# A written-out drain, one gather buffer per batch, and the maximum's scores first, in a one-core attention and mixture-of-experts kernel

## The reference

```python
x = x + tanh(g_xattn[0]) * attention(layernorm(x), ctx, ctx)     # 16 batches, 256 x 256, 16 heads of 16
xf = layernorm(x)                                                # 4096 tokens of 256
scores = softmax(xf @ w_router);  weights, indices = top_k(scores, 2)      # 8 experts
moe    = sum over the two experts of weight * (silu(xf @ w1) * (xf @ w3)) @ w2   # hidden 512
shared = silu(xf @ ws1) * (xf @ ws3) @ ws2
x = x + tanh(g_ffn[0]) * (shared / 3 + moe * 2 / 3)
```

## Time and profile before

| | |
|---|---|
| runs | 934.19, 934.75, 927.93 us, median 934.19 |
| profiled execution | 931.92 us |
| its span (first to last instruction) | 930.2 us |
| mean granted clock of PE | 0.948 |
| busy | PE 818.6 (88%), PEld 727.7, DVE 535.9 (58%), ACT 418.0 (45%), POOL 378.9 (41%) |

### The profile page before, as it was taken

How to read it: one execution, slowest core, us unless ns; L and a number is a source line. 1 busy time by engine, 2 the same in 40 slices (tenths; PEclk the granted TensorE clock), 3 DMA queues, 4 the chain that set the end, 5 groups by cost and what they waited for, 6 DMA issues and landing times.

```text
span 930.2 us, 19000 instructions
## 1 busy us (share of the span) xinstructions
PE 818.6 (88%) x7106; PEld 727.7 (78%) x7107; DVE 535.9 (58%) x1104; ACT 418.0 (45%) x691; POOL 378.9 (41%) x373
## 2 busy tenths in 40 slices
PE   2478999999999998878899999999999999968765
PEld 2365777677777766558799999999999999968765
DVE  4256788888888878554843444444343433535545
ACT  5228776666666655644333333333333333311211
POOL 4524446555555532325660513135051300345571
PEclk9759999999999989789999999999999999988887
DMA  4869877778888886324575413143241111234352
GB/s 147 236 129 190 202 165 209 191 189 186 206 197 191 172 172 170 132 93 164 181 250 196 133 57 124 56 124 112 69 132 60 56 57 45 86 97 129 122 153 73
DMA packets 103409, 131.47 MB, mean 141 GB/s; under 512 B 9904, under 2 KB 87472, under 8 KB 103344
## 3 DMA queue, kind: packets, MB, share of 16 engines
q1 hardware_dynamic: 91696, 93.37, 40.3%
q0 software_dynamic: 11648, 37.23, 12.1%
HBM read 75.25 MB, written 55.05 MB: 140 GB/s over the span
## 4 chain that ended last, share of the span: by engine, by line
PE 62%; DVE 18%; issue 8%; DMA 3%; ACT 3%; another core or an unknown queue 3%; SPq 1%; POOL 1%; DVEq 0%; ACTq 0%; POOLq 0%
PE bank L499 7%; PE bank L501 6%; PE bank L500 6%; DVE row_max L1178 6%; PE bank_sm L499 5%; PE bank_sm L501 5%; PE bank_sm L500 5%; PE bank_ss L499 4%; PE bank_ss L501 4%; PE bank_ss L500 4%; PE bank_sm L592 4%; PE bank_ss L581 3%; PE bank L608 3%; PE bank L517 2%
## 5 line engine op out<-in xcount | busy, mean ns | idle before, releaser
L1178 DVE TENSOR_REDUCE row_max<-bank_sm 128x4 f32<-128x1024 f32 x128 | 156.3, 1221 | 70.3 <-PE bank_sm L592 47.1
L820 ACT ACTIVATE probs_T<-bank_ss 128x1024 f32<-128x1024 f32 x128 | 131.6, 1028 | 38.7 <-PE bank_ss L581 37.3
L499 PE MATMUL bank_sm<-xg_h,w_h 128*128 128x256 f32 x400 | 119.9, 300 | 30.7 <-DVE xg_l L1052 27.6
L1052 DVE TENSOR_TENSOR gT_l<-gg,gT_h 128x1024 fp32r<-128x1024 f32 x50 | 80.8, 1616 | 95.2 <-ACT gT_h L946 90.7
L501 PE MATMUL bank_sm<-xg_l,w_h 128*128 128x256 f32 x400 | 118.6, 296 | 0.0
L500 PE MATMUL bank_sm<-xg_h,w_l 128*128 128x256 f32 x400 | 118.4, 296 | 0.0
L499 PE MATMUL bank<-w_h,gT_h 128*128 128x256 f32 x400 | 114.6, 287 | 3.2 <-DVE x_all L1289 3.2
L499 PE MATMUL bank_ss<-xg_h,w_h 128*128 128x256 f32 x400 | 116.8, 292 | 0.0
L501 PE MATMUL bank<-w_l,gT_h 128*128 128x256 f32 x400 | 114.3, 286 | 0.7 <-issue 0.7
L500 PE MATMUL bank<-w_h,gT_l 128*128 128x256 f32 x400 | 114.6, 286 | 0.4 <-issue 0.4
L500 PE MATMUL bank_ss<-xg_h,w_l 128*128 128x256 f32 x400 | 113.1, 283 | 0.0
(11 more groups left out here) (173 smaller groups left out, 2015.0 us busy)
## 6 DMA issues: line engine op xcount, KB each, us to landing
qk_d<-qk_s SPq DMA_DIRECT2D x32, 512.0 KB, 7.7
w_raw<-wall POOLq DMA_DIRECT2D x27, 512.0 KB, 3.9
k<-qk_d SPq DMA_DIRECT2D x96, 128.0 KB, 4.4
q<-qk_d SPq DMA_DIRECT2D x96, 128.0 KB, 6.4
xg<-xs_d SPq DMA_DIRECT2D x35, 256.0 KB, 2.7
ys_d<-y_s SPq DMA_DIRECT2D x34, 256.0 KB, 2.2
x<-x SPq DMA_DIRECT2D x16, 256.0 KB
c_s<-ctxT SPq DMA_DIRECT2D x16, 256.0 KB, 3.2
```

What stands on the lines that cost most here:

```text
L499: pe.matmul(out, ah, bh, start=first and k == 0, stop=False)
L820: act.activation(pT[:, 2 * (pv % 4):2 * (pv % 4) + 2, :].rearrange("p h t -> p (h t)"), SS[:, :], ACT.Exp, scale=D ** -0.5).then_inc(exp_o ...
L1052: return v.tensor_tensor(dst, ps, high.bitcast(F32), ALU.subtract)
L1178: v.tensor_reduce(mx[B.slot][:, :, :].rearrange("p t (r q) -> p r t q", r=2)[:, :, :, p], SM[:, :].rearrange("p (r t k) -> p r t k", r=2, ...
```

## The change

- **Order of the drain.** `iterations` now ends at i = NB - 1. What is left of the batches 13, 14 and 15 (x13, x14, x15) is written out in a row on each engine, with the pieces of the shared tiles between them; the tables UP1, UP3 and DOWN go. For that the steps became functions of their own.
- **Work moved out of the drain.** ACT's copy w_h0 is at i = NB - 3, DVE's `w_l` and the first `xg_l` are in slots 0 to 3 of i = NB - 1. `router_exp` of the last three batches, and the sums of scores and router weights that need it, come behind tile 6's g_high and g_low (three buffers instead of one hold their input and output). POOL's cut of the first expert's weights has its last part behind the last scatter.
- **Slots.** PE issues the maximum's scores first, the exponential's second.
- **Router on DVE.** slot_i is cast ahead of slots_all; score_sum, its reciprocal and the weights come at the end, each waiting for the one before.
- **Gathers.** `yg` has room for all 16 batches (in the place of the experts' weights, which are used up), with a semaphore for each batch. The 64 gathers are issued in a row, with one `carry`.
- **Mixes and SP's queue.** The mixes come one tile later: 0 and 1 in tile 9, 12 and 13 in tile 15. Ahead of the stores of tile j - 2's mixes stands the load of tile j, so the loads run a tile further ahead.

```diff
-    for i in range(-AHEAD, NB + 3):
+    for i in range(-AHEAD, NB):
...
 def mixed_at(j):
-    if j == NB - 1:
-        return ()
-    first = 2 * (min(j, NB - 1) - EARLY - 2)
-    return range(max(0, first), NB if j == NB else max(0, first + 2))
+    first = max(0, 2 * (min(j, NB) - EARLY - MIX_FROM))        # MIX_FROM = 3
+    return range(first, min(NB, max(0, 2 * (j + 1 - EARLY - MIX_FROM))) if j < NB else NB)
...
 SP
     for j in range(EARLY + 2, NB):
         load_shared(j, total + (j - 1))
-        for b in mixed_at(j - 1):
+        for b in mixed_at(j - 2):
             store_out(b)
...
 PE
         for p in range(PAIRS):
-            scores(p)
+            if B:
+                scores_to_max(B, p)
+            V, pv = late_pair(C, S, p)
+            if V:
+                scores_to_exp(V, pv)
...
+    scores_to_exp(x15, PAIRS - 2)
+    values(x15, 2)
+    up1(0, SHARED)
+    scores_to_exp(x15, PAIRS - 1)
+    logits(x13)
+    values(x15, 3)
+    project_out(x14)
+    rank(x13, rk_tail)
+    attention_rows(x15)
+    up3(0, SHARED)
+    turn_out(x15)
+    turn_norm(x14)
+    up1(1, SHARED)
+    logits(x14)
+    project_out(x15)
+    rank(x14, rk_tail)
+    up3(1, SHARED)
+    down(0, SHARED)
+    turn_norm(x15)
+    up1(2, SHARED)
+    logits(x15)
+    up3(2, SHARED)
+    rank(x15, rk_tail)
+    down(1, SHARED)
...
 ACT
+            if i == SPLIT_AT and p in (1, 3, 5):               # SPLIT_AT = NB - 3
+                n = p // 2
+                act.wait_ge(w_in[n], 16)
+                act.activation(w_h0[:, part(n)], wraw[:, part(n)], ACT.Copy).then_inc(w_used, 1)
...
+    for b in (x13, x14, x15):
+        router_exp(b)
...
 DVE
+            if i == NB - 1 and p in (0, 1, 3):
+                n = (0, 1, None, 2)[p]
+                v.wait_ge(w_used, n + 1)
+                v.tensor_tensor(w_l0[:, part(n)], wraw[:, part(n)], w_h0[:, part(n)].bitcast(F32), ALU.subtract).then_inc(w_ok, 1)
+            if i == NB - 1 and p == 2:
+                x_low_shared(0, 0)
...
     def mix(b):
-        n, turn = b % RG, b // RG
-        v.wait_ge(yg_in[n], turn * 64 + 64)
+        v.wait_ge(yg_in[b], 64)
...
 POOL
+    scatter(x14)
+    cut(1, 0, which=(0, 1))
+    scatter(x15)
+    cut(1, 0, which=(2,))
...
+    carry(NB)
     for b in range(NB):
-        n = b % RG
-        moved(po, mix_ok, b - RG + 1)
-        carry(NB + b)
         for t in range(TS):
-            for k, dst in enumerate((yga, ygb)):
+            for k in range(2):
                 po.indirect_dma_start(
-                    out=dst[n][:, t, :], out_offset=None, in_=ys_d,
+                    out=yg[:, b, k, t, :], out_offset=None, in_=ys_d,
```

More of the change, by code:

```diff
@@ L219, in build @@
             ysh = sb(m, "y_shared", [P, EARLY, TS * E])
[L221 to L226, removed]
+            with ExitStack() as w:
+                w_h, w_l = [], []
+                for i in range(2):
+                    w_h.append(sb(w, f"w_h{i + 1}", [P, WSZ], F32R))
+                    w_l.append(sb(w, f"w_l{i + 1}", [P, WSZ], F32R))
+                w_h.append(w_h0)
+                w_l.append(w_l0)
+            yg = sb(m, "y_gathered", [P, NB, 2, TS, E])
             x2a = sb(m, "x2_all", [P, NB, TS * E])
@@ new lines, in scores_to_exp @@
+            def scores_to_exp(V, pv):
+                if pv == 0:
+                    pe.wait_ge(mrow, V.n(32, 32))
+                moved(pe, exp_ok, V.n(PAIRS, pv))
+                for half in range(TC):
+                    for par in range(2):
+                        own = slice(ROWS * par, ROWS * par + ROWS)
+                        r = pe.matmul(SS[:, par * 512 + half * L:par * 512 + (half + 1) * L],
+                                      k4[V.slot][own, pv, half * P:(half + 1) * P], q4[V.slot][own, pv, :],
+                                      start=True, stop=True)
+                r.then_inc(ss_ps, 1)
@@ new lines, in scores_to_max @@
+            def scores_to_max(B, p):
+                if p == 0:
+                    pe.wait_ge(stk[B.slot], B.turn * 192 + 192)
+                moved(pe, mx_ok, B.n(PAIRS, p))
+                for half in range(TC):
+                    for par in range(2):
+                        own = slice(ROWS * par, ROWS * par + 3 * D)
+                        r = pe.matmul(SM[:, par * 512 + half * L:par * 512 + (half + 1) * L],
+                                      q4[B.slot][own, p, half * P:(half + 1) * P], k4[B.slot][own, p, :],
+                                      start=True, stop=True)
+                r.then_inc(sm_ps, 1)
@@ new lines, in turn_out, with project_out, turn_norm @@
+            def turn_out(S):
+                pe.wait_ge(o_ok, S.n(1, 1))
+                transposes(T0, o_s, oT_ps)
+            def project_out(S2):
+                weights(S2, 3)
+                pe.wait_ge(oTl_ok, S2.n(1, 1))
+                for t in range(TC):
+                    project_rows(T1, t, oT_h, oT_l, wo_h, wo_l, op_ps)
+            def turn_norm(S2):
+                pe.wait_ge(xn2_ok, S2.n(1, 1))
+                pe.wait_ge(x2_ok, S2.n(1, 1))
+                transposes(T1, xn2_s[S2.slot], xn2T_ps)
@@ L1106, in before @@
[L1106 to L1108 removed]
+                        norm(S2)
                 def behind(p):
@@ L1276, in _ @@
             g_low(EARLY)
+            for b in (x13, x14, x15):
+                score_sum(b)
+                score_weights(b)
             with v.Fori(EARLY + 1, last) as g:
@@ L1336, in load_w, with cut @@
                 po.dma_start(wraw[:, part(i)], wall[WALL[k]][:, part(i)]).then_inc(w_in[i], 16)
-            def cut(k, p, tiles=None):
-                for i in range(WP):
+            def cut(k, p, tiles=None, which=range(WP)):
+                for i in which:
                     po.wait_ge(w_in[i], 16 * (k + 1))
@@ L1395, in one @@
                 if S3:
-                    po.wait_ge(slot_ok, S3.n(1, 1))
-                    carry(S3.b)
-                    for t in range(TC):
-                        for k in range(2):
-                            po.indirect_dma_start(
-                                out=xs_d, out_offset=bass.IndirectOffsetOnAxis(ap=slot_i[:, t, k:k + 1].bitcast(U32), axis=0),
-                                in_=xn2_s[S3.slot][:, t, :], in_offset=None).then_inc(sc_done, 16)
+                    scatter(S3)
                 if Eb and Eb.b == 1:
```

563 lines of the change are left out of this document (291 added, 272 removed).

## The result

The changed kernel takes 955.56 us (median of four, 952.7 to 959.27), the kernel before 932.29: a ratio of 1.0257 with a 95% interval of 1.0201 to 1.0313. It is slower by 2.6%, where 895 was forecast. The profiled execution took 955.6 us, its span is 953.8.

The account below looks back on a forecast made before the run. The tail was taken as a loop through four engines without PE, the drain as PE waiting for DVE, the iterations as PE-busy. From the 930.2 us span, -27 - 12 + 2 = 893, plus 1.7 gives 895; range 875 to 920.

Parts of the forecast that it names:

- Part by part: the tail: Tail: loads and gathers leave the loop, pitch 8.9 us; PE's path ends at 897.7, gathers' at 903.1; gain 27 us.
- rivals of 0.13 and 0.12: Tail: PE's signals held again and again, 7.0 us each, time 918 (0.13), or held until the last gather, 955 (0.12).
- rival (b): Tail: PE's signals held until the last gather, tile 9's `xg_l` at 886.4 instead of 821.10, time 955; chance 0.12.
- the groups of eight: Tail, gathers behind the first twelve: no late signal shows, but none falls more than 5 us behind a group's start.
- The tail's own sum: Tail: pitch 8.9 us, gathers 1.47 us apart, the gathers' path ending the kernel at 903.1, 27 us gained.
- the three waits of PE that were named: Drain: PE waits for DVE 5.8 us for `xg_l`, 3.2 for `mask_total`, 1.8 for the logits' order, 10.8 in all.
- 12 - 2 = 10: Before the tail: 12 us gained in the drain, less 2 lost in the iterations to DVE's router sums.
- the drain's term: Drain: 10.8 us of PE's waits gone and 1.2 for less time at the lower clock, 12 us gained (4 to 24).
- 0 for the swap: Iterations: issuing the maximum's scores first changes nothing, 0 us, with bounds -12 and +14.
- (c): Iterations: the swapped scores cost PE's slack, +14 us, time 909; chance 0.07.
- The router's links: Iterations: DVE's second sum has its links in a row, 0.15 us an iteration, +2 us in all.
- Rival (d): Tail: mixes wait for gathers too, 3 us more of DVE a tile, pitch 11.5, time 905; chance 0.03.

Follow-up runs that it names:

- e3: Changed kernel with mixes and SP's queue ordered as in the kernel before, the 64 gathers still in one row: 977.6 us, ratio 1.0511 to the kernel before.
- e14: Changed kernel with the exponential's scores issued first again, as before: 952.59 us, ratio 1.0245 to the kernel before, signals late.
- e10: Changed kernel run again unchanged, signals prompt: 883.47 us, ratio 0.9718 to the kernel before.
- e4: Changed kernel with mixes, SP's queue and the gathers' waits as in the kernel before: 921.78 us, ratio 0.992 to the kernel before.
- e13: Changed kernel with only the first expert's rows gathered and used twice, 32 gathers, signals prompt: 869.98 us, ratio 0.957 to the kernel before.
- e19: Changed kernel with the 64 gathers replaced by plain DMAs on POOL's queue, signals late: 884.75 us, ratio 0.9549 to the kernel before.

## Why the prediction was wrong

- **The step that failed** is the forecast's silent one in "Part by part: the tail": that PE's path stays as in the earlier trace rows while 64 gathers run beside it. The pause at tile 9 was read, but priced as something that happens once (7 us), with its return as rivals of 0.13 and 0.12. The runs show in its place a hold about as long as the row: the step to tile 10 took 70.9 us instead of 8.9, and the gathers' end was no longer what mattered. That is rival (b), whose working gave a span of 953 and a time of 955. Measured: 953.8 and 955.6. That they agree so closely is partly luck: the hold began a tile later than I had it (signals of one more tile got through, in 19.6 us), and `xg_l` behind it came 10 us later (886.41, where 886.4 less the 10 us of drain and iterations was worked out). Nor are the signals kept back until the last gather, as (b) has it: some come through inside the row (e3, e14). Both cases that the trace of before showed had pointed to it, since the wait ended with the gathers; what I held against it, ACT's signal at 811.85, was itself 1.2 us behind its matmul. A pattern seen in both places where a signal fell late enough deserved more than 0.12.
- **What the groups of eight could tell** I had said myself: none of their signals fell late enough to be tested. From "nothing shows" I still took the likeliest case.
- **The tail's own sum was right**, where the hold is absent. Prompt, the tail from its first gather to the end of the span is 883.5 - 786.3 = 97.2 us, forecast 903.1 - 803.05 = 100.05; the pitch 8.54 (8.9 was taken); gathers 1.40 us (1.47). The gathers end the kernel, as said. Against it, the tail of the kernel before lost its 7 us there too: 910.1 - 789.8 = 120.3 instead of 127.2. So the tail's gain is 23 us there, not 27, and the whole change gives 26 (909.31 to 883.47) where 37 were forecast.
- **The drain** lost the three waits of PE that were named (10.8 to 2.1 us), but 5.6 us of waiting for DVE came back behind them, where the tables of the routed tiles now stand ahead of an `xg_l`. The forecast had no term for it. The first gather came 9.9 us earlier, where 12 - 2 = 10 was forecast, but by two errors. At the end of iteration 12 (the `oT_l` at 335.09, before 336.37) the changed kernel is 1.3 us ahead, and what lies between there and the first gather gave 8.6. Prompt, the first gather comes 3.5 us earlier (789.8 to 786.3): 4.4 behind at that place (334.46 and 330.09), and 7.9 from there on. So the drain's term was 8 to 9 instead of 12. In time, e4 shows 8.75 for both together (930.53 to 921.78).
- **The iterations**: 0 for the swap was wrong. It costs 0.25 to 0.3 us in each, some 3 to 4 us in all; PE meets its wait for row_max earlier, as (c) said, at a quarter of its price. The router's links may cost the 0.2 that remain; that isn't shown. In the late condition the iterations came out 0.3 us shorter all the same, for a reason that stays open.
- Rival (d) falls: in the prompt condition, where mixes and gathers meet (e10, mixes of tile 9 from 811.12 to 814.6 beside the gathers of 811.67 and 813.12), a pair keeps its 0.87 to 0.88 us. The changed kernel's late trace can't tell, since all its mixes came after the last gather. Rival (e) falls: SP issues four loads in a row before the first stores (783.96 in e10), and a tile takes 8.54 us.

## What to carry to other kernels

Before a row of indirect DMAs is made longer beside a busy PE, look in the trace for signals that arrive late at the end of the longest row there is, and price the change as if the hold lasts as long as the row. A wait that looks like a mere shortage of buffers can be what keeps two engines apart: when it goes, put the gap back on purpose (here 2.6 us for eight gathers), or, where the rows allow it, use plain DMAs. When a wait is taken out of a stage, look at the waits just behind it too: here 5.6 of 10.8 us came back there. And run both kernels at different times before believing a sign: this change is 2.6% slower in one condition and 2.8% faster in the other.

## What the runs showed of the hardware that was not expected

- In some groups of runs PE's signals are late beside POOL's indirect DMAs, in others never; the median of the kernel before is then 926 to 932 or 906 to 910 us. It isn't fixed to a chip: one and the same chip ran e10 to e13 prompt and e19 late. What sets it is open. Each of these executions was recorded (it has its span and granted clock), so whether the recording has a part in the delay no run tells either.
- In the late condition, beside a row of 64 gathers, one signal came 64 us behind its matmul and the next 32, and PE started one matmul in 2.8 us, without a wait for another engine that the profile shows. It recovered within some 10 us of the last gather. With plain DMAs in their place, 265 GB/s in one row of 34 us, nothing was late. Whether a queue of PE's outgoing signals is what fills up was only argued.
- A gather that starts while DVE works with two SBUF inputs waits until that instruction ends (1.93 instead of 0.96 us); DVE doesn't wait for the gather (`gT_l` inside one: 1.22 us, as elsewhere).
- No version that gathers all rows was found that is best in both conditions: with pauses 908.8 (late) and 897 to 903 (prompt), without them 955.6 and 883.5. With pauses the changed kernel is ahead of the kernel before in both, by little where signals are prompt (0.9771; 0.987 and 0.9946).
